# Routing 8192 tokens to pairs of experts: places from products on TensorE, logits from the unscaled residual, an earlier first product

## The chip, the cores and the metric

One core of a Trainium2 chip runs the whole program. The metric is the device time in microseconds (us) of one execution.

## What is computed

Input: 8 sequences of 1024 rows of 128 channels. A frequency-domain attention and convolution block gives a residual; its layer norm is the input of a mixture of eight experts, and a second layer norm gives the output. For the change only the routing matters:

```python
x = _layernorm(x + attn(x))                       # 8192 rows, D = 128
d2 = sum(xs*xs) + sum(centroid*centroid) - 2*(xs @ centroid.T)
dist = sqrt(maximum(d2, 1e-12))
w, sel = top_k(dist, 2); w = softmax(w)           # the two farthest centroids
we[row, sel] = w
for e in range(8):
    h = silu(xs @ Wg[e] + bg[e]) * (xs @ W1[e] + b1[e])
    out += we[:, e:e+1] * (h @ W2[e] + b2[e])
x = _layernorm(x + out)
```

## The kernel before, in words

**Phase 1** (`phase1`, lines 161 to 994) works batch by batch (8 batches of 8 tiles of 128 rows), as a software pipeline whose last part is a `tail()` on each engine. The normed rows go to `rows_dram`, their transposes times the centroids give the logits `lg`, and GpSimd gives the squared norms `sq`. Each engine has its own program in an order written out by hand, with counting semaphores between them; an engine waits in order, and everything behind a wait waits too. VectorE's tail (lines 863 to 928) runs: the first of the two top-one searches over the 48 tiles of batches 0 to 5 (`top_two`, line 1014), residual and statistics of the last batch (L892 to L899), an inverse root by a Newton chain of small linked operations (L901 to L909), four of the eight scalings of the last batch (L913; ScalarE does the other four, L703), copies, the second search, the one-hots `OH` of the 28 pairs of experts (`pair_rows`, L1048 to L1058), then for three chunks of 16 tiles a scan and a rank (`pair_sums` L1070, L1071; `pair_ranks` L1078 to L1080). In the loop GpSimd makes the inverse root (L971 to L983). SP stores the rows (L325, L327).

**Routing** (`route`, L1083 to L1341) is the first part of phase 2, a block that starts when all engines have ended phase 1. VectorE: both searches for the last 16 tiles, their pair one-hots, the last scan and rank, the running totals of the pairs (L1170, L1171), which tile holds rows of which pair (L1172 to L1175), each row's place (L1193 to L1202), the step tables' one-hots (L1205 to L1213), then in four quarters one-hots of the place's high and low part (L1225 to L1228). TensorE multiplies these, which inverts the permutation (L1327); `steptab` (L1240 to L1245) and `idx` (L1251) come out, and `placed` is signalled. GpSimd builds the rows' weights `we` (L1281 to L1284), splits the biases into a high and a low part (L1287, L1289), stores and reloads them into row 127 of the weights (L1292, L1296), then waits for `placed` and gathers the first four tiles (L1302). SP stores `we` (L1341). VectorE waits for all of these stores ahead of `idx`.

**Experts** (`experts`, L1354 on): tile k of the permuted rows is gathered by GpSimd four steps ahead, transposed on TensorE (L1478), copied by ScalarE into `xT` (L1538), split by ScalarE into `xh` (L1522) and by GpSimd into `xl` (L1425). A step t does two units (a tile with an expert): products for gate and value (`up`, L1447), Silu (L1533), product h (L1620), transposes (L1455), products down (L1465), accumulation (L1631). Offsets of a step are loaded from `steptab` into each engine's registers. The order on TensorE in a step is: transpose of tile t+2, gate products, value products, transposes of step t-1, down products of step t-2. So transposes 0, 1 and 2 stand ahead of the first product.

## Time and profile before

| | |
|---|---|
| median of 3 runs (lowest, highest) | 600.55 us (600.13, 600.82) |
| profiled execution: its time, its span | 602.22 us, 600.2 us |
| mean granted TensorE clock | 0.93 |
| busy over the span: TensorE, weight load | 507.4 us (85%), 477.5 us (80%) |
| busy: VectorE, ScalarE, GpSimd | 395.2 (66%), 341.3 (57%), 287.3 (48%) |
| moved by DMA in the first of 40 slices | 231 GB/s |

The page's picture of 40 slices of 15 us, in tenths:

```profile
PE   3868999999998540087999999999999999999990
DVE  2579879889989888981334346555564646666663
POOL 0132534544553100615444444577777777754443
PEclk9979989999999855578999999999999999999996
```

Slices 0 to 13 are phase 1, 14 to 17 its tail and the routing, the rest the experts. An engine's digit is its busy share of the slice, PEclk the granted clock. PE is TensorE, PEld its weight load, DVE VectorE, ACT ScalarE, POOL GpSimd, SP the sync engine; an engine's name with a q is its queue.

### The profile page before, as it was taken

To read this page: it belongs to the slowest core of one execution; us is meant where nothing else is said; L and a number is where in the kernel's file an instruction comes from. 1 tells how busy PE (TensorE), PEld (TensorE's weight loads), DVE (VectorE), ACT (ScalarE), POOL (GpSimd) and SP (SyncE) were. 2 spreads that over 40 slices of the span, in tenths; PEclk is the share of its full clock that TensorE was granted. 3 is DMA by queue.
4 is the path that set the end of the run, shared out by engine and by line. 5 is a ranking of instruction groups with operands and counts; after the bars stand their busy time and mean duration, and the time that the engine had idled before them with its cause. 6 is when DMAs were issued, how large, how long until landed. Compare 5 with 4: busy or idle time off the path is not lost.

```text
span 600.2 us, 13796 instructions
## 1 busy us (share of the span) xinstructions
PE 507.4 (85%) x4090; PEld 477.5 (80%) x4090; DVE 395.2 (66%) x1121; ACT 341.3 (57%) x721; POOL 287.3 (48%) x414
## 2 busy tenths in 40 slices
PE   3868999999998540087999999999999999999990
PEld 3766887887887430076999999999999999999990
DVE  2579879889989888981334346555564646666663
ACT  3366868878877402035555555666666575755661
POOL 0132534544553100615444444577777777754443
PEclk9979989999999855578999999999999999999996
DMA  8241246146232110201000000111111111100000
GB/s 231 66 128 49 51 115 162 45 121 163 78 85 72 35 35 2 21 9 24 20 20 20 20 18 18 29 33 35 35 39 33 34 37 38 35 26 19 19 23 31
DMA packets 48975, 31.16 MB, mean 52 GB/s; under 512 B 14251, under 2 KB 46582, under 8 KB 48918
## 3 DMA queue, kind: packets, MB, share of 16 engines
q1 hardware_dynamic: 43974, 20.87, 13.6%
q0 software_dynamic: 4224, 8.75, 5.3%
q10 hardware_dynamic: 720, 0.82, 0.5%
q8 instruction: 31, 0.51, 0.3%
q14 instruction: 26, 0.21, 0.1%
HBM read 21.73 MB, written 8.69 MB: 51 GB/s over the span
## 4 chain that ended last, share of the span: by engine, by line
PE 52%; DVE 3%; issue 3%; POOL 2%; DMA 1%; POOLq 0%; ACT 0%; DVEq 0%
PE ps L1447 25%; PE ps L1465 17%; PE ps L1455 8%; PE ps L1478 1%; DMA bias_parts<-blo 1%; POOL wo L1282 0%; DMA xs<-rows_dram,idx 0%; POOL we L1284 0%; POOL out_dram L1414 0%; POOL blo L1289 0%; POOL xs L1302 0%; POOL bhi L1287 0%; DVE Lc L1071 0%; POOL we L1281 0%; DVE xs L1631 0%
## 5 line engine op out<-in xcount | busy, mean ns | idle before, releaser
L1447 PE MATMUL ps<-wts,xh 128*128 x620 | 154.2, 332 | 1.3 <-issue 1.2
L1620 DVE TENSOR_TENSOR h<-ps,sg 128x684 f32<-128x684 f32 x78 | 67.6, 866 | 91.1 <-PE ps L1447 90.8
L1465 PE MATMUL ps<-w2s,hT 115*128 (+1 forms) x930 | 116.5, 274 | 0.3 <-DVE xs L1631 0.3
L1425 POOL TENSOR_TENSOR xl<-xT,xh 127x128 fp32r<-127x128 f32 x155 | 67.9, 457 | 98.6 <-ACT xh L1522 98.5
L1465 PEld LDWEIGHTS ps<-w2s,hT 115*128 115x128 f32 (+1 forms) x930 | 109.9, 191 | 0.6 <-issue 0.6
L1447 PEld LDWEIGHTS ps<-wts,xh 128*128 128x128 f32 x620 | 104.6, 191 | 1.8 <-issue 1.7
L1447 PE MATMUL ps<-wts,xl 128*128 x310 | 99.4, 321 | 0.0
L1533 ACT ACTIVATE sg<-ps 128x684 f32<-128x684 f32 x78 | 57.7, 739 | 67.2 <-PE ps L1447 67.2
L1542 ACT ACTIVATE hT<-ps 114x768 f32<-114x768 f32 x78 | 63.0, 808 | 56.5 <-PE ps L1455 56.5
L1631 DVE SCALAR_TENSOR_TENSOR xs<-ps,xs 128x128 f32 x155 | 54.3, 351 | 50.6 <-PE ps L1465 47.6
L1414 POOL DMA_INDIRECT out_dram<-xs,idx x64 | 62.9, 982 | 25.8 <-issue 17.6
L1455 PE MATMUL ps<-cr,h 128*114 128x128 f32 x465 | 63.4, 272 | 0.3 <-issue 0.3
L1410 POOL DMA_INDIRECT xs<-rows_dram,idx x60 | 58.1, 969 | 9.1 <-issue 4.4
L1447 PEld LDWEIGHTS ps<-wts,xl 128*128 128x128 f32 x310 | 58.8, 190 | 0.0
L1455 PEld LDWEIGHTS ps<-cr,h 128*114 128x114 f32 x465 | 54.5, 134 | 2.3 <-issue 0.5
L1522 ACT ACTIVATE xh<-xT 127x128 fp32r x155 | 39.1, 301 | 2.0 <-ACT xT L1538 0.9
L742 DVE SCALAR_TENSOR_TENSOR YI<-XF,dw,YI 128x432 f32<-128x432 f32 (+5 forms) x48 | 37.0, 772 | 0.6
L967 POOL TENSOR_TENSOR Pb<-Sb,rs 128x512 f32<-128x512 f32 x16 | 19.2, 1198 | 28.7 <-DVE rs L830 28.6
L742 DVE SCALAR_TENSOR_TENSOR YR<-XF,dw,YR 128x448 f32<-128x448 f32 (+5 forms) x48 | 30.9, 644 | 1.7
L1507 ACT ACTIVATE xs<-xs,nrm,y 128x128 f32<-128x128 f32 x64 | 27.8, 483 | 7.3 <-DVE nrm L1603 7.3
L971 POOL TENSOR_TENSOR y<-ve,cm 128x8 f32<-128x8 f32 x7 | 11.6, 1664 | 37.8 <-DVE vh L763 37.8
L961 POOL TENSOR_TENSOR wts<-st,wts 128x684 f32 (+1 forms) x8 | 13.1, 1640 | 27.8 <-ACT wts L636 27.8
(280 smaller groups left out, 870.3 us busy)
## 6 DMA issues: line engine op xcount, KB each, us to landing
xt<-_attn_hidden_states_dram SPq DMA_DIRECT2D x8, 512.0 KB, 6.0
xres<-_attn_hidden_states_dram SPq DMA_DIRECT2D x7, 512.0 KB, 5.3
rows_dram<-x1s SPq DMA_DIRECT2D x7, 512.0 KB, 3.7
w2s<-in_L_ffn_W_dram SPq DMA_DIRECT2D x8, 171.0 KB
st<-in_L_ffn_Wg_dram SPq DMA_DIRECT2D x8, 171.0 KB, 3.1
st<-in_L_ffn_W_dram SPq DMA_DIRECT2D x8, 171.0 KB, 3.6
stl<-in_L_ffn_Wg_dram SPq DMA_DIRECT2D x8, 171.0 KB, 3.7
stl<-in_L_ffn_W_dram SPq DMA_DIRECT2D x8, 171.0 KB, 4.2
```

The costliest lines, as they stand in the source:

```text
L742: ins = v.scalar_tensor_tensor(out=y[:, :, k:n], in0=src, scalar=w, in1=y[:, :, k:n], op0=ALU.mult, op1=ALU.add)
L1410: v.indirect_dma_start(xs[:, k, 0:RD], None, rows, bass.IndirectOffsetOnAxis(idx[:, k:k + 1], 0)).then_inc(gat[k % GATS], 16)
L1414: v.indirect_dma_start(out_rows, bass.IndirectOffsetOnAxis(idx[:, k:k + 1], 0), xs[:, k, 0:D], None).then_inc(s["scattered"], 16)
L1425: v.tensor_tensor(xl[0:D - 1, i % 2, u, :], xT[0:D - 1, bass.ds(off[u], P)], xh[0:D - 1, i % 2, u, :].bitcast(F32), ALU.subtract).then_inc ...
L1447: mm = pe.matmul(ps[:, 2 * w + u, 0:HF], a[:, t % 2, u, :], wflat[:, bass.ds(w1[u] + (b + w * HF), HF)], start=(k == 0), stop=(k == 2))
L1455: mm = pe.transpose(ps[0:HG, 4 + u, k * P:(k + 1) * P], h[:, t % 2, u, k * HG:(k + 1) * HG], ident)
L1465: mm = pe.matmul(ps[:, low(t) + u, 0:D], hT[0:n, t % 2, u, k, :], w2flat[0:n, bass.ds(w1[2 + u] + k * D, D)], start=(k == 0), stop=(k == 2))
L1522: nc.scalar.activation(xh[0:D - 1, i % 2, u, :], xT[0:D - 1, bass.ds(off[u], P)], ACT.Copy).then_inc(s["xh_done"], 1)
L1533: nc.scalar.activation(sg[:, 0:units(t), :], ps[:, 0:units(t), 0:HF], ACT.Silu).then_inc(s["sg_done"], 1)
L1542: nc.scalar.activation(hT[0:HG, b % 2, 0:n, :, :].rearrange("p u k m -> p u (k m)"), ps[0:HG, 4:4 + n, 0:3 * P], ACT.Copy).then_inc(s["hT_ ...
L1620: v.tensor_tensor(h[:, t % 2, 0:units(t), :], ps[:, 2:2 + units(t), 0:HF], sg[:, 0:units(t), :], ALU.mult).then_inc(s["h_done"], 1)
L1631: v.scalar_tensor_tensor(out=row, in0=ps[:, low(c) + u, 0:D], scalar=xsflat[:, bass.ds(off[2 + u], 1)], in1=row, op0=ALU.mult, op1=ALU.add ...
```

## The change

- **Places.** Ranks and totals no longer come from scans. TensorE multiplies `OH` by a triangle (rank within a tile), by a vector of ones (counts of each tile), and by the identity (its transpose `oht`); small products of the counts give totals and each (pair, tile)'s first place, split in two two-byte parts and spread into `R`, and `oht` times `R` gives each row's first place. Pairs are laid out in rounds, so four multiplications make `OH` in place of nineteen. Tables of need and of steps are made with products too. Most constants are packed as two-byte numbers, and all but the first 137 columns are loaded later, on SP.
- **Last batch.** TensorE transposes and multiplies the unscaled residual `xt`; the scale and the mean are applied to the logits (`nc8`). GpSimd makes the inverse root. ScalarE scales all eight tiles into `xlast`. The second search and the pair one-hots of the 48 tiles follow the statistics at once. ScalarE makes the early tiles' square roots.
- **Moved.** Weights of the rows in two parts (48 and 16 tiles), on GpSimd for more of their steps; the bias split to GpSimd's tail of phase 1 and its stores to SP; three memsets from VectorE to GpSimd; `idx` ahead of the tables (`tabled`); waits for the stores from VectorE to GpSimd.
- **First product.** Transposes 1 and 2 follow the first gate and value products; three gathers go ahead instead of four.

```diff
+def pair_columns():
+    return [tuple(sorted((a, (a + d) % E))) for d in range(1, E // 2 + 1) for a in range(E if d < E // 2 else E // 2)]
...
@@ phase1, SP @@
+                if X and not Y:
+                    sp.dma_start(cr[:, g["c2"]["gblk"][0]:], g["cst2"][:, g["c2"]["gblk"][0]:]).then_inc(rest_in, 16)
+                    sp.dma_start(braw[:, 0:HF], g["bg"]).then_inc(s["bias_in"], 16)
+                    sp.dma_start(braw[:, HF:], g["b1"]).then_inc(s["bias_in"], 16)
...
+                for k, part in enumerate((bhi, blo)):
+                    sp.wait_ge(s["bias_split"], k + 1)
+                    sp.dma_start(parts[k], part[:, :].bitcast(F32)).then_inc(bias_out, 16)
+                sp.wait_ge(bias_out, 32)
+                for k in range(2):
+                    sp.dma_start(wts[D - 1:D, :, 2 * k * HF:2 * (k + 1) * HF].bitcast(F32), parts[k:k + 1]).then_inc(bias_out, 16)
                 sp.wait_ge(s["last_x1"], TB)
-                sp.dma_start(rows_t[B - 1][:, :, 0:D], xres[:, :, :]).then_inc(s["rows_out"], 16)
+                sp.dma_start(rows_t[B - 1][:, :, 0:D], xlast[:, :, :]).then_inc(last_out, 16)
...
-            sp.wait_ge(s["rows_out"], 16 * B)
+            sp.wait_ge(rows_out, 16 * (B - 1))
@@ TensorE @@
-            pe.matmul(ps[:, 6, 0:E], ones[:, :], cT2[:, :], start=True, stop=True).then_inc(s["prep_mm"], 1)
+            pe.matmul(ps[:, 6, 0:E], ones[:, :], cT2[:, :], start=True, stop=True)
+            pe.matmul(ps[:, 6, E:2 * E], ones[:, :], cT[:, 0:E], start=True, stop=True).then_inc(s["prep_mm"], 1)
...
+                for h in range(2):
+                    pe.wait_ge(s["zs_done"], 2 * (B - 1) + h + 1)
+                    for j in range(4):
+                        mm = pe.transpose(ps[:, h, j * P:(j + 1) * P], xt[:, 4 * h + j, :], ident)
+                    mm.then_inc(s["t_done"], 1)
@@ ScalarE, tail @@
+                act.wait_ge(w_early, 1)
+                for m, root in ((g["m1"], g["s1"]), (g["m2"], g["s2"])):
+                    nc.scalar.activation(root[:, 0:EARLY * CT], m[:, 0:EARLY * CT], ACT.Sqrt).then_inc(s["sqrt_early"], 1)
                 act.wait_ge(s["last_rstd"], 1)
+                for j in range(TB):
+                    nc.scalar.activation(xlast[:, j, :], xt[:, j, :], ACT.Identity, bias=nl[:, j:j + 1], scale=yl[:, j:j + 1]).then_inc(s["last_x1"], 1)
@@ VectorE, tail, behind the statistics @@
+                v.tensor_scalar(vl[:, :], mvl[:, :, 1], EPS, None, ALU.add).then_inc(s["last_seed"], 1)
+                v.tensor_scalar(vhl[:, :], mvl[:, :, 1], EPS, 0.5, ALU.add, ALU.mult).then_inc(s["last_seed"], 1)
+                top_two(nc, g, 0, EARLY * CT, link, True)
+                dve.sem_inc(w_early, 1)
+                pair_rows(nc, g, 0, EARLY, link)
...
+                link(v.tensor_tensor(last, ps[:, 6, 0:TB * E].rearrange("p (j e) -> p j e", j=TB), yl[:, :].unsqueeze(2).broadcast_to((P, TB, E)), ALU.mult))
+                v.tensor_tensor(last, last, nc8[:, :, :], ALU.add).then_inc(s["lg_ev"], 1)
@@ GpSimd, tail, behind squares(B - 1) @@
+                pool.wait_ge(s["bias_in"], 32)
+                v.tensor_copy(bhi[:, :], braw[:, :]).then_inc(s["bias_split"], 1)
+                pool.wait_ge(s["bias_split"], 1)
+                v.tensor_tensor(blo[:, :], braw[:, :], bhi[:, :].bitcast(F32), ALU.subtract).then_inc(s["bias_split"], 1)
+                pool.wait_ge(s["last_seed"], 2)
+                v.tensor_tensor(yl[:, :], vl[:, :], cm[:, :], ALU.pow).then_inc(s["last_root"], 1)
...
@@ pair_rows @@
+    for d in range(1, E // 2 + 1):
+        w = E if d < E // 2 else E // 2
+        ins = v.tensor_tensor(OH[:, c0:c1, at:at + w, :], maskT[:, 0:w, lo:hi].rearrange("p a (c t) -> p c a t", t=CT),
+                              maskT[:, d:d + w, lo:hi].rearrange("p a (c t) -> p c a t", t=CT), ALU.mult)
@@ route, VectorE @@
+            dve.wait_ge(s["tri_cp"], EARLY)
+            link(v.tensor_tensor(prod[:, 0:EARLY, :, :], trs[:, :, :, :], OH[:, 0:EARLY, :, :], ALU.mult))
+            dve.wait_ge(s["counts"], 2)
+            v.tensor_copy(cntb[:, EARLY, :], cnt[:, EARLY * BLK:]).then_inc(s["counts_cp"], 1)
...
+            dve.wait_ge(s["firsts"], 1)
+            link(v.tensor_copy(hl[:, :, 0], V))
+            link(v.tensor_tensor(hl[:, :, 1], V, hl[:, :, 0], ALU.subtract))
...
             for k in (14, 7):
-                link(v.tensor_tensor(posm[:, :, 0:k, :], posm[:, :, 0:k, :], posm[:, :, k:2 * k, :], ALU.add))
+                link(v.tensor_tensor(prod[:, :, 0:k, :], prod[:, :, 0:k, :], prod[:, :, k:2 * k, :], ALU.add))
...
+            dve.wait_ge(s["places"], 1)
@@ in the quarters @@
+                if c == 1:
+                    dve.wait_ge(s["upto"], 1)
+                    link(v.tensor_tensor(upos[:, :], upto, need[:, :], ALU.mult))
+                    v.tensor_tensor(uhot[:, :, :], short("unit").unsqueeze(1).broadcast_to((P, 4, UPAD)), upos[:, :].unsqueeze(2).broadcast_to((P, 4, UPAD)),
+                                    ALU.is_equal).then_inc(s["unit_hot"], 1)
...
@@ route, ScalarE @@
+            for c in range(EARLY):
+                act.wait_ge(s["tri"], c + 1)
+                nc.scalar.activation(trs[:, c, :, :].rearrange("p a t -> p (a t)"), ps[:, 2 + c, 0:NPAIR * CT], ACT.Copy).then_inc(s["tri_cp"], 1)
+            for c in range(EARLY):
+                turned(c, (0, 1, 6)[c])
+            act.wait_ge(s["late"], 1)
+            for m, root in ((m1, s1), (m2, s2)):
+                nc.scalar.activation(root[:, TE:NT], m[:, TE:NT], ACT.Sqrt).then_inc(s["sqrt"], 1)
...
@@ route, GpSimd @@
+            weights(0, 0, TE, s["weights_early"])
+            pool.wait_ge(s["weights_early"], 1)
+            v.memset(xh[96:P, :, :, :].bitcast(F32), 1.0).then_inc(prep, 1)
...
+            weights(1, TE, NT, s["weights_late"])
@@ route, TensorE @@
+            for c in range(EARLY):
+                mm = counts(c)
+            mm.then_inc(s["counts"], 1)
+            for c in range(EARLY):
+                tri(c, 2 + c)
+            for c in range(EARLY):
+                turned(c, (0, 1, 6)[c])
...
+            totalled(0, EARLY)
...
@@ experts @@
+            pool.wait_ge(weights_out, 16 * B)
+            pool.wait_ge(rows_out, 16 * (B - 1))
+            pool.wait_ge(last_out, 16)
+            pool.wait_ge(placed, 1)
+            for k in range(GATS - 1):
+                gather(k)
...
+                if t < 0 or t >= 1:
+                    if t != -1:
+                        turn_in(k)
...
                     up(t, 0, w1[t]).then_inc(s["g_done"], 1)
+                if t == 0:
+                    turn_in(1)
```

The functions that the diff calls: `counts(c)` is four products of one column, `turned(c, bank)` four of 128, `tri(c, bank)` one of 448, `totalled` four of one column for each chunk, all of two-byte data; `weights(k, lo, hi, done)` is w2, two weightings and their sum for the tiles lo to hi; `turn_in(k)` waits for gather k and transposes tile k.

## Rows read from the trace of the kernel before

**Rows 1.** Windows: start and end, width, busy us (x instructions) per engine, granted clock, DMA.
```profile
280.00:600.00 320.00, 304.95 (x2366) 302.50 (x2364) 172.03 (x528) 184.19 (x429) 185.36 (x272) 0.98 0.10 28
```

**Rows 2.** Waits from 196 to 282 us: total, times, longest.
```profile
POOL xs L1302 <- DVE idx L1251: 11.3, 1, 11.3
```

**Rows 3.** Timeline of VectorE: start, us, line, operation, out<-in [idle before].
```profile
204.34 0.64 DVE L899 BATCH_NORM_AGGREGATE mvl<-bn 128x2 f32<-128x6 f32 x8
...
210.64 0.55 DVE L1031 SCALAR_TENSOR_TENSOR dist<-oh,dist 128x384 f32<-128x384 f32 x1
...
214.17 0.86 DVE L1048 TENSOR_TENSOR maskT<-oh 128x384 bf16<-128x384 f32 x1
...
227.76 0.90 DVE L1080 TENSOR_REDUCE rank<-rtmp 128x16 f32<-128x448 f32 x1
229.20 0.29 DVE L1033 TENSOR_TENSOR dist<-lg,cn 128x128 f32<-128x128 f32 x1 [0.54 <-PEq L176]
...
267.54 0.23 DVE L1251 SCALAR_TENSOR_TENSOR idx<-inv 128x64 uint32<-128x64 f32 x1
```

**Rows 4.** Timeline of VectorE, one two-byte comparison of a quarter.
```profile
256.10 1.21 DVE L1226 TENSOR_TENSOR lohot<-io,lob 128x2048 bf16<-128x2048 bf16 x1
```

**Rows 5.** Timelines of GpSimd and VectorE where they meet.
```profile
95.51 1.64 POOL L961 TENSOR_TENSOR wts<-st,wts 128x684 f32 x1 [1.63 <-ACT wts L636]
...
95.92 1.68 DVE L742 SCALAR_TENSOR_TENSOR YI<-XF,dw,YI 128x416 f32<-128x416 f32 x1
...
249.96 1.61 POOL L1289 TENSOR_TENSOR blo<-braw,bhi 8x684 fp32r<-8x684 f32 x1
...
250.25 1.41 DVE L1197 TENSOR_TENSOR pos<-pos,rank 128x64 f32<-128x64 f32 x1
```

**Rows 6.** Timeline of GpSimd: the inverse root in the loop, and weights.
```profile
108.00 1.64 POOL L971 TENSOR_TENSOR y<-ve,cm 128x8 f32<-128x8 f32 x1 [5.23 <-DVE vh L763]
...
112.68 0.20 POOL L983 TENSOR_TENSOR nmr<-c,ya 128x8 f32<-128x8 f32 x1
...
242.84 1.07 POOL L1281 TENSOR_TENSOR we<-oh,r_w 128x512 f32<-128x512 f32 x1 [6.36 <-DVE r_w L1186]
243.87 2.85 POOL L1282 TENSOR_TENSOR wo<-oh,r_w 128x512 f32<-128x512 f32 x1
```

**Rows 7.** Timeline of ScalarE: a switch of tables, scalings, copies out of PSUM.
```profile
95.30 1.28 ACT L639 ACT_TABLE_LOAD   x1
96.60 0.63 ACT L639 ACTIVATE Sb<-Sb 128x512 f32<-128x512 f32 x1
...
198.70 3.18 ACT L694 ACTIVATE x1s<-xres,nmr,y 128x128 f32<-128x128 f32 x8
202.69 1.09 ACT L698 ACTIVATE x1T<-ps 128x512 f32<-128x512 f32 x2 [0.81 <-PE ps L513]
```

**Rows 8.** Timeline of TensorE: two-byte products of 156 and of 128 columns.
```profile
255.64 3.28 PE L1319 MATMUL ps<-uhot,ulhs 64*1 64x156 bf16 x24 [12.32 <-DVE ulhs L1213]
...
265.06 2.05 PE L1327 MATMUL ps<-hihot,lohot 128*128 128x128 bf16 x16 [0.27 <-DVE hihot L1228]
```

**Rows 9.** The stores of `we` on SP: timeline, and the line's landing times.
```profile
248.82 5.12 SPq L1341 DMA_DIRECT2D rows_dram<-we  x8
...
DMA to landing us min/median/max: 2.2/3.0/3.8
```

**Rows 10.** Start of the experts: timelines of TensorE and ScalarE, a window.
```profile
270.72 0.33 PE L1478 MATMUL ps<-cr,xs 128*128 128x128 f32 x1 [1.78 <-DMA xs<-rows_dram,idx]
...
274.81 0.93 PE L1447 MATMUL ps<-wts,xh 128*128 x2 [1.17 <-issue]
...
276.92 0.74 ACT L1533 ACTIVATE sg<-ps 128x684 f32<-128x684 f32 x1 [2.05 <-PE ps L1447]
...
274.00:277.00 3.00, 2.19 (x8) 2.20 (x9) 0.00 (x0) 0.95 (x2) 1.56 (x3) 0.56 0.10 25
```

**Rows 11.** Timeline of TensorE in the prologue.
```profile
15.91 0.60 PE L344 MATMUL ps<-cT,ones 128*128 128x8 f32 x2 [1.55 <-ACT cT L566]
```

More of the change, by code:

```diff
@@ new lines, in resident_constants @@
+    twice = twice.copy()
+    twice[:, 0:NPAIR] += np.eye(NPAIR)
+    twice[:, 32:32 + NPAIR] += np.eye(NPAIR)
+    parts["glast"] = rows_of(twice)
+    first, end = np.full((64, P), BIG), np.full((64, P), -BIG)
+    inc = np.zeros((64, E // 2))
+    for h in range(2):
+        r = slice(32 * h, 32 * h + NPAIR)
+        first[r, 64 * h:64 * h + NT] = np.arange(NT) * P
+        end[r, 64 * h:64 * h + NT] = np.arange(NT) * P + P
+        for p, pair in enumerate(cols):
+            for e in pair:
+                if e // 4 == h:
+                    inc[32 * h + p, e % 4] = 1
@@ L109, in resident_constants @@
+    parts["io4"] = halves(np.tile(np.repeat(np.arange(P), 4), (P, 1)).astype(float))
+    parts["tiles"] = halves(np.tile(np.arange(NT), (P, 1)).astype(float))
     return parts
@@ L1264, in _ @@
[L1264 removed]
+                act.wait_ge(s["high"], c + 1)
+                nc.scalar.activation(hihot[:, part, 0, :, :], hieq[:, part, :, :], ACT.Copy, scale=con("part")).then_inc(s["high_place"], 1)
         @block.gpsimd
```

611 lines of the change are left out of this document (311 added, 300 removed).

## The prediction, made before the changed kernel was run

> **What bounds the kernel now.** I read the page first, then stretches, waits and the timeline of each engine between the two phases. In the experts' phase TensorE is busy for 305 of 320 us at a granted clock of 0.98 (2.4 GHz nearly throughout) [rows 1]: the change leaves that loop alone, so those 320 us stay. Between the phases TensorE is mostly idle, and the wait that ends last is GpSimd's for `idx`: 11.3 us on VectorE [rows 2]. So the path is VectorE's. Its timeline [rows 3] gives the landmarks: statistics of the last batch end at 204.98, its scans and ranks end at 228.66, the routing block starts at 229.20, and `idx` is written at 267.77. A microsecond taken out of that chain is a microsecond of span. The profiled execution took 602.22 us (span 600.2); the median of the runs shown is 600.55, so I subtract 1.67 at the end.
>
> **Tail of phase 1, on VectorE.** Removed from it: the Newton chain of twelve small operations, four scalings, the copy of x1T, three scans with nine following operations. Added: two seeds (0.25), one second logits operation. What is left behind the statistics is the second top-two of 48 tiles, 214.17 - 210.64 = 3.53 us, the mask (0.86, and about 0.35 for its three repeated rows), four pair products in place of nineteen small ones (384 two-byte elements at the rate of the 2048-element comparison, 1.21 us or 0.57 ns each [rows 4], plus 0.1: about 1.1 together) and two logits operations, 0.6. That would end at 204.98 + 0.25 + 3.53 + 1.2 + 1.1 + 0.6 = 211.7.
>
> **What the moved bias split costs there.** GpSimd now does it behind its squares, at about 198, beside VectorE's first top-two. The trace shows what such a meeting costs: a VectorE operation on 416 elements with two SBUF inputs, which should be near the 0.55 us of 384 elements [rows 3], takes 1.68 when GpSimd's 1.64 us subtraction started before it, and the addition of 64 elements takes 1.41 because it has to let `blo` end at 251.57 [rows 5]. The second is the very operation that is moved, so its 1.61 us falls on the top-two almost whole: I take 1.7 us for the pair, with 0 (they miss) and 2.75 (both whole, with the 1.14 of `bhi`'s cast taken into the bound as an estimate of the same kind of width) as ends. Statistics then end at 206.7 and VectorE's phase at 213.4.
>
> **The last rows go over ScalarE and SP.** The inverse root is GpSimd's now. In the loop the same seven operations take from 108.00 to 112.88, 4.9 us [rows 6], so bias and scale are ready at 206.95 + 4.9 = 211.85. VectorE's second top-two ends at 210.5, and ScalarE's two early square roots behind it are done by 211.1 (about 0.25 each), so they cost nothing; their cover is the root chain. Then ScalarE scales all eight tiles alone: eight such operations took 3.18 [rows 7], until 215.1. SP issues the row store (0.4) and the block ends; its landing is no longer waited for here. With the 0.5 us that the boundary took before (228.66 to 229.20), the routing block starts at 216.0 against 229.2. **ScalarE, not VectorE, sets this end.** The two bias stores and loads are on SP before it, behind 201, and have 10 us to land; without that cover they would cost two trips of some 3 us. The transposes and logit products of the last batch run unscaled while VectorE is in the statistics.
>
> **Routing block, VectorE's order, counted from its start.** Top-two of 16 tiles: fourteen operations of 0.29 with 0.03 between them, 4.5; signal and pair rows 1.3: 5.8. Now a wait: ScalarE must have copied three triangular products. TensorE makes twelve counts, three products of 448 columns, twelve turned blocks and twelve totals; a small two-byte product costs 0.137 in a run of 24 and 0.128 in one of 16 [rows 8], I take 0.12 for the narrower ones: 1.45 + 1.1 + 1.45 + 1.45, so the totals are there at 5.6, and ScalarE's three copies at half a microsecond each (two of 512 columns took 1.09 [rows 7]) end at 7.5. VectorE stalls 1.7. Early products 1344 elements 0.85, counts copy 0.2, reciprocal 0.4, last total after four more products 0.7, late products 0.65 (PSUM input, 448 elements at the 1.2 ns of the 384-element operation, 0.55 [rows 3], plus start): 10.4. The first places need eight single-precision passes, here 0.12 each: 11.3, a stall of 0.9. Split 0.4, spread 0.55, bounds and presence 0.45, two halvings 0.9, reduction 0.95, reciprocal 0.2, five operations to `lob` 1.0: 15.7. Between the first places and the reduction, TensorE makes sixteen place products (2.0) and ScalarE turned blocks, bounds and weights, all hidden by the halvings; if they are late, the place addition waits. The four quarters of one-hots are as before, 4096 elements each at 0.57 ns, 9.4: 25.1. Within them the presence, `upos` and `uhot` cost 0.95, and a wait for `upto`, which stands behind the first sixteen inverse products, 0.7: 26.8. The last sixteen inverse products 2.05 [rows 8] with latency 2.3, copy and `idx` 0.55: 29.65. The tables (1.7) come behind `idx` and run beside the first gather.
>
> The old block took 267.77 - 229.20 = 38.6. Gone are its scan and ranks, the wide base product with its single-precision halvings, half of the one-hot units, and the tables ahead of `idx`.
>
> **GpSimd's weights beside it.** Differences, products, eight-wide weights and the memsets taken from VectorE now run from about 11.4 of this block (the late square roots stand on ScalarE behind its three copies, three turned blocks, 1.65, and a switch of tables, 1.3), meeting VectorE's two-input operations. Alone GpSimd's list is some 6.5 us: for the early 48 tiles three wide steps of 0.85 and two small ones, four memsets of up to 0.5, and the same for 16 tiles. Half as much again for the meetings, and the weights end at about 21; their stores, 0.64 each and 3.8 to land at worst [rows 9], at about 26, under the 32 of `idx`.
>
> So `idx` stands at 216.0 + 29.65 + 2.5 = 248.15 in place of 267.77: 19.6 us saved, 13.2 in the tail of phase 1 and 6.4 in routing.
>
> **First product.** It stood 274.81 - 267.77 = 7.04 behind `idx`, the first transpose 2.95 behind it, and 1.17 went into loading offsets after the third [rows 10]. Now it needs the first tile only: 2.95 + 0.3 + 1.2, about 4.45. But the second transpose comes behind its first half, and ScalarE does copy, split and a table load of 1.28 before the Silu, which before was ready and waited for TensorE at 276.92. That Silu comes 9.2 to 10.1 behind `idx`, ended 9.8 before. Of the 2.6 us on TensorE I therefore count 0.5; ends 2.6 saved and 1 lost (the fourth gather is now issued behind the first subtraction).
>
> **Prologue.** A product more (two passes, 0.60 for two [rows 11]) adds up to 0.6 ahead of the first transforms; 278 KB less of constants to load ahead of the first transposes gives back up to 1.2, at the 231 GB/s of the page's first slice. I take 0.3 saved, with 0.6 lost and 0.9 saved as ends. The rest of the constants, three SP issues in the first step of the loop, lies beside compute.
>
> **Sum.** 602.2 - 19.6 - 0.5 - 0.3 = 581.8 in the profiled execution, 580.1 for the median; I say 580.
>
> **Table loads, trace against notes.** In the loop the load starts at 95.30 and the Exp behind it at 96.60 [rows 7]: 1.30 us for a switch, nothing more. That price is in the steps above. By the Trainium skill (ScalarE: Activation LUTs, What ACT_TABLE_LOAD costs) a switch is a load of 1283 ns and a drain of about 1380 ns; the row does not show the drain.
>
> **Rivals.** (1) *The forecast's path*, 580, likeliest: 0.67.
> (2) *GpSimd's weights end last.* If each of its steps goes at 2.85 for 1.07, its 6.5 us become 17.5, from 227.4 to 244.9, and the stores land 5.1 later at 250.0, 1.9 behind my `idx`: 582. For it, the row of 2.85; against it, that blocking is mutual and VectorE waits often in this block. 0.12.
> (3) *The early first product counts whole.* The granted clock was 0.56 from 274 to 277 [rows 10], against 0.98 over the experts' phase [rows 1], after the lull before the first product. If the lull is short enough for full clock to hold, the first half step takes 0.9 less and all of the start counts: 577. 0.11. The rows do not say which.
> (4) *A switch costs load and drain.* Two switches stand ahead of the bounds and the late weights, one ahead of the Silu: if a switch blocks for a second stretch as long as its load, 1.28 more each, and half of it hides: 582. The switch row nearly excludes it: 0.01. (The page named above gives this mechanism.)
> (5) *Slower.* The weights of (2), starved at the port, stretched by more than 5.4: from 227.4, 6.5 x 5.4 + 5.1 us of stores reach 267.6, where `idx` was. Above that factor the kernel is slower than before; at a factor of 6 they land at 271.5, which gives 603. The dearest ratio in the trace is 2.7: 0.03.
> (6) *Same mechanism, dearer hops*: some dozen crossings between engines that I priced at 0.1 or less cost 0.5 to 1 each, single-precision rates on the new two-byte operations: 588 to 596, 0.05.
> (7) *It does not shorten the path*: something else held the experts back. Nothing in the waits says so: 0.01.
>
> **Range and chances.** Downward, from 580: the split misses (1.7), no blocking in routing (2.5), start whole (2.1), prologue (0.6): 573. Upward: blocking whole (1.1 and 1.9), two-byte operations at single-precision rate (2.2), hops (1.2), start and prologue (2.4): 589. That holds (1) to (4) and part of (6). A measurement of this kernel tells about 0.2% from no change. Faster 0.96: all but (5) and (7); same 0.01; slower 0.03.
>
> **What would show it.** Right: the routing block starting near 216 behind eight ScalarE scalings; VectorE's first top-two with one operation of about 2 us; a stall of about 1.7 before the early product; `idx` near 248 and first product 4.5 behind it; TensorE's loop of experts unchanged. Wrong: a block start set by VectorE or SP; GpSimd's first gather waiting for `we` stores; `hieq` quarters longer than 2.4 us; a lower clock in the experts' phase.

## The result, and the profile after

The changed kernel takes 583.12 us (median of 4 runs, 580.71 to 584.92), the one before 600.68 us on the same chip (4 runs, 600.13 to 602.06): a ratio of 0.9717, 95% interval 0.9684 to 0.9749, 17.6 us less. Predicted were 580 us and a range of 573 to 589. The profiled execution took 584.92 us, its span is 582.4 us, its mean granted clock 0.93.

| stretch of the profiled executions, us | before | after | predicted change | measured change |
|---|---|---|---|---|
| start to VectorE's last `VT` | 196.53 | 199.39 | -0.3 | +2.86 |
| tail: to the routing block's first operation | 32.67 | 18.80 | -13.2 | -13.87 |
| routing: to the end of `idx` | 38.57 | 29.69 | -6.4 | -8.88 |
| start: to the transpose of tile 5 | 17.79 | 19.38 | -0.5 | +1.59 |
| experts behind it, to the end | 314.6 | 315.1 | 0 | +0.5 |
| span | 600.2 | 582.4 | -20.4 | -17.8 |

These five stretches, read from the timelines of VectorE and TensorE, are used for every kernel below. The tail and routing together gave 22.75 us where 19.6 were predicted; phase 1 and the start took back 4.45.

The busy tenths of the profile's page, in 40 slices of 14.6 us:

```profile
PE   3768989999999856769999999999999999999990
DVE  1569778899899888813434447464645556666663
POOL 0142525545535533054454454776776776754453
PEclk9769889999999965689999999999999999999996
```

TensorE's lull between the phases had digits of 5, 4, 0, 0 and now has none below 5. New, and not a matter of the edit as far as one sees here: the third digit of PEclk is 6, the granted clock fell in the prologue.

**Tail.** Timeline of VectorE in the changed kernel (start, us, line, operation, shapes, idle before):

```profile
199.39 0.46 DVE L944 SCALAR_TENSOR_TENSOR VT<-ps,al,xln 128x64 f32<-128x64 f32 x2 [1.09 <-PE ps L572]
...
200.98 0.93 DVE L1115 TENSOR_SCALAR dist<-dist 128x384 f32<-128x384 f32 x1
201.95 0.55 DVE L1116 TENSOR_REDUCE r_m<-dist 128x48 f32<-128x384 f32 x1
202.53 1.28 DVE L1117 TENSOR_TENSOR eq<-dist,r_m 128x384 f32<-128x384 f32 x1
...
215.63 0.23 DVE L981 TENSOR_TENSOR lg<-lg,nc 128x64 f32<-128x64 f32 x1
218.19 0.29 DVE L1113 TENSOR_TENSOR dist<-lg,cn 128x128 f32<-128x128 f32 x1 [2.34 <-PEq L236]
```

Timeline of GpSimd beside it:

```profile
200.95 0.74 POOL L1041 CAST bhi<-braw 8x684 fp32r<-8x684 f32 x1
201.78 1.62 POOL L1043 TENSOR_TENSOR blo<-braw,bhi 8x684 fp32r<-8x684 f32 x1
...
213.24 0.69 POOL L1058 TENSOR_TENSOR nl<-c,yal 128x8 f32<-128x8 f32 x1
```

And of ScalarE:

```profile
213.97 3.18 ACT L780 ACTIVATE xlast<-xt,nl,yl 128x128 f32<-128x128 f32 x8 [0.68 <-POOL nl L1058]
218.14 1.28 ACT L1293 ACT_TABLE_LOAD   x1 [0.99 <-PEq L236]
219.44 0.24 ACT L1293 ACTIVATE r_ew<-r_df 128x48 f32<-128x48 f32 x1
...
222.38 1.37 ACT L1308 ACTIVATE trs<-ps 128x448 bf16<-128x448 f32 x3
```

Two operations of the first search are long, each while one of the two halves of the bias split is under way; the reduction between them, at 0.55, is not. VectorE is through at 215.86 and then idle for 2.34 us; ScalarE's eight scalings end last, at 217.15, and the block begins 1.04 later, with SP's issue of the row store (0.41 us from 217.18) in between.

**Routing.** VectorE again, to be set against [rows 3 to 5]:

```profile
223.88 0.85 DVE L1212 TENSOR_TENSOR prod<-trs,OH 128x1344 bf16<-128x1344 bf16 x1
...
227.73 0.18 DVE L1225 CAST hl<-ps 112x16 bf16<-112x16 f32 x1 [1.50 <-PE ps L1406]
...
228.15 1.37 DVE L1227 TENSOR_TENSOR R<-hl,cr 112x512 bf16<-112x512 bf16 x1
229.45 1.01 DVE L1231 TENSOR_SCALAR mxs<-cr,bb 64x128 f32<-64x128 f32 x1
...
233.44 0.42 DVE L1243 TENSOR_SCALAR hii<-posi 128x64 int32<-128x64 int32 x1
...
239.42 0.16 DVE L1267 TENSOR_TENSOR upos<-ps,need 128x4 bf16<-128x4 f32 x1
...
247.66 0.22 DVE L1273 SCALAR_TENSOR_TENSOR idx<-inv 128x64 uint32<-128x64 f32 x1
```

The early product has no idle time before it: its inputs are ready. The one real stall is 1.50 us, for the first places. `upos` does not wait for `upto` either: the products for it end at 239.39, 0.03 ahead.

**Start of the experts.** Timelines of GpSimd, TensorE and ScalarE in the order of time, and three windows (start and end, width, busy us of each engine, granted clock, DMA), to be set against [rows 10]:

```profile
248.87 1.18 POOL L1526 DMA_INDIRECT xs<-rows_dram,idx  x1 [14.17 <-DVE idx L1273]
...
253.18 0.90 PE L1569 MATMUL ps<-wts,xh 128*128 x2 [1.11 <-ACT xh L1658]
...
256.62 1.28 ACT L1669 ACT_TABLE_LOAD   x1
...
257.92 0.74 ACT L1669 ACTIVATE sg<-ps 128x684 f32<-128x684 f32 x1
...
258.93 0.30 PE L1578 MATMUL ps<-cr,xs 128*128 128x128 f32 x1 [1.78 <-ACT sg L1669]
```

```profile
254.00:256.00 2.00, 2.00 (x9) 1.94 (x8) 0.00 (x0) 0.28 (x1) 0.96 (x1) 0.50 0.16 41
...
258.00:260.00 2.00, 1.07 (x7) 1.10 (x8) 0.87 (x1) 1.34 (x4) 1.14 (x3) 1.00 0.14 35
260.00:262.00 2.00, 2.00 (x10) 1.93 (x9) 0.00 (x0) 0.91 (x2) 1.27 (x2) 0.54 0.00 0
```

The first product stands 5.3 us behind the end of `idx` in place of 7.04, but the Silu behind it 10.04 in place of 9.15: a table load stands directly ahead of it, and TensorE then waits 1.78 us for it. The first gather begins 0.99 us behind `idx`; before it was 0.28.

Three questions followed: whether the change lengthened phase 1, what the start's parts are, and whether the blocked operations of tail and routing are what I took them for.

### The profile page after: what moved, and what is told of

Same layout as the page of the kernel before. It is cut to its first block, busy times and chain, and to the rows that moved or that the text cites. A ratio compares the mean times of both kernels' runs of the same rounds, so it can differ in the third digit from the quotient of the medians.

```text
span 582.4 us, 13894 instructions
## 1 busy us (share of the span) xinstructions
PE 514.3 (88%) x4161; PEld 486.5 (84%) x4161; DVE 371.0 (64%) x1045; ACT 350.7 (60%) x743; POOL 289.1 (50%) x422
## 3 DMA queue, kind: packets, MB, share of 16 engines
q0 software_dynamic: 4096, 8.66, 5.5%
## 4 chain that ended last, share of the span: by engine, by line
PE 55%; DVE 4%; issue 1%; ACT 1%; DMA 0%; POOL 0%; DVEq 0%; ACTq 0%; POOLq 0%
PE ps L1569 25%; PE ps L1594 17%; PE ps L1584 9%; PE ps L1578 1%; PE ps L1427 1%; DMA xs<-rows_dram,idx 0%; DVE lohot L1257 0%; POOL out_dram L1530 0%; PE ps L1441 0%; PE ps L1406 0%; DVE hieq L1256 0%; DVE xs L1763 0%; ACT xs L1641 0%; DVE R L1227 0%; DVE hihot L1259 0%
## 5 line engine op out<-in xcount | busy, mean ns | idle before, releaser
L1530 POOL DMA_INDIRECT out_dram<-xs,idx x64 | 62.9, 982 | 26.2 <-issue 17.5
L1526 POOL DMA_INDIRECT xs<-rows_dram,idx x64 | 62.4, 975 | 23.9 <-DVE idx L1273 14.2
L1019 POOL TENSOR_TENSOR Pb<-Sb,rs 128x512 f32<-128x512 f32 x16 | 19.2, 1199 | 28.7 <-DVE rs L902 28.6
```

The source lines that it names most:

```text
L1526: v.indirect_dma_start(xs[:, k, 0:RD], None, rows, bass.IndirectOffsetOnAxis(idx[:, k:k + 1], 0)).then_inc(gat[k % GATS], 16)
L1530: v.indirect_dma_start(out_rows, bass.IndirectOffsetOnAxis(idx[:, k:k + 1], 0), xs[:, k, 0:D], None).then_inc(s["scattered"], 16)
```

## The experiments

Each starts from the changed kernel, unless it says otherwise. Spreads are lowest to highest run; the kernel before ran beside each of them and stood at 599.93 to 600.63 us. The groups ran on different chips, so medians of different groups are compared only roughly.

| kernel | median, us (runs; spread) | ratio to before, 95% interval | to `VT` | tail | routing | start | span |
|---|---|---|---|---|---|---|---|
| the change again | 583.83 (6; 578.9 to 585.1) | 0.9717 [0.9679, 0.9756] | 195.45 | 18.82 | 29.67 | 17.94 | 577.0 |
| transposes as before | 579.82 (6; 579.0 to 582.5) | 0.9668 [0.9635, 0.9701] | 193.03 | 18.80 | 29.69 | 19.44 | 576.1 |
| Silu table early | 577.23 (6; 574.3 to 579.8) | 0.9606 [0.9572, 0.9640] | 196.49 | 18.80 | 29.71 | 17.13 | 577.0 |
| Silu early, tables held back | 577.52 (5; 576.8 to 578.7) | 0.9609 [0.9584, 0.9633] | 195.92 | 18.81 | 29.66 | 16.58 | 575.9 |
| idle products | 575.64 (6; 574.7 to 576.8) | 0.9587 [0.9556, 0.9618] | 191.54 | 18.80 | 29.70 | 19.32 | 574.4 |
| the kernel before, idle products | 596.66 (7; 595.9 to 597.5) | 0.9936 [0.9913, 0.9959] | 191.19 | 32.68 | 38.57 | 18.10 | 595.4 |
| bias split earlier | 579.37 (4; 578.7 to 583.6) | 0.9673 [0.9632, 0.9714] | 195.46 | 17.51 | 29.69 | 17.99 | 575.8 |
| and scalings shared | 578.33 (4; 578.1 to 580.8) | 0.9631 [0.9598, 0.9663] | 198.83 | 16.97 | 29.68 | 17.54 | 577.9 |
| constant weights | 577.24 (4; 574.3 to 581.5) | 0.9598 [0.9552, 0.9644] | 197.68 | 18.81 | 27.79 | 19.20 | 578.6 |
| Silu, split, scalings | 574.43 (5; 573.7 to 575.2) | 0.9558 [0.9534, 0.9583] | 194.19 | 16.99 | 29.70 | 16.99 | 572.6 |
| and idle products | 571.09 (6; 570.3 to 572.8) | 0.9504 [0.9480, 0.9527] | 192.36 | 16.98 | 29.70 | 17.18 | 570.9 |
| and gathers placed as before | 571.99 (6; 570.7 to 572.6) | 0.9527 [0.9488, 0.9567] | 192.07 | 16.98 | 29.69 | 16.75 | 570.2 |

The stretches are of the profiled execution alone. Tail and routing repeat within 0.05 us; the time to `VT` lies between 193.0 and 199.4 in the six profiles of kernels whose phase 1 is the same, and the start scatters too. Medians of kernels without idle products therefore carry that draw, and an edit is judged by its stretch first.

### Was phase 1 longer because of the change?

The change, run again without an edit:

> The changed kernel itself, unedited, as the measure for the three kernels beside it. Its four runs so far lie between 580.71 and 584.92 us, a spread of 4.2, while the kernel before spreads by 0.7 in its first three. Theory A: the spread is TensorE's clock. In the profiled run the granted clock was 0.50 from 18 to 24 us and 0.55 from 39 to 42, where the kernel before had 1.00, and phase 1 came out 2.86 us later at the first operation of its tail. Then runs with a fast prologue have that operation near 196.5 and runs with a slow one near 199.4, and the rest (tail, routing, start) agrees within 0.5 us. Theory B: the later prologue is work that the change added (a product, a later load) and is there in every run. Expected median 583, range 580.5 to 585.

Its stretch to `VT` was 195.45, 3.9 less than in the first profile and 1.1 less than before the change. So the 2.86 us are mostly not the change's. The start did not repeat within the expected 0.5: 17.94 for 19.38.

What goes with the time to `VT` is the granted clock, in two places. The first batch's statistics come at 60.2 to 64.6 us in the six profiles of this phase 1, with granted clocks of 0.50 to 0.89 in the two windows shown below. From there to the second batch's it takes 23.4 to 23.7 us where the granted clock from 80 to 100 us is 0.91 to 0.94 (four of the six, and the kernel before), and 21.5 to 21.7 where it is 1.00 (two). Behind that every profile of every kernel takes 21.6 us for each of the next four batches: all of the scatter of phase 1 lies ahead of about 110 us.

Next, idle products on TensorE, in two gaps of the prologue:

```diff
+            for _ in range(8):
+                pe.matmul(ps[:, 7, 0:P], ident, ident, start=True, stop=True)
             pe.wait_ge(s["prep_cp"], 10)
...
+                if Y and not T:
+                    pe.wait_ge(s["v_ev"], 2)
+                    for _ in range(6):
+                        pe.matmul(ps[:, 7, 0:448], ident, cs[:, 0:448], start=True, stop=True)
```

> TensorE gets idle products in two gaps of the prologue: eight of 128 columns behind the preparing transposes and six of 448 columns ahead of the first transposes of step 1; nothing reads them. Theory A (the later and more scattered prologue is the clock's doing): the clock stays at 1.00 from 15 to 60 us, the first operation of the tail comes at 196.5 or earlier, 2 to 4 us are saved and the spread of the runs falls to under 1 us. Theory B (the prologue is later because of added work): the clock stays up but the tail starts within 0.5 us of 199.4.

The same lines in the kernel before the change:

> The kernel before the change, with the same idle products in the two gaps of the prologue as in e_warm (eight of 128 columns, six of 448; nothing reads them). In e_warm the first operation of the tail came at 191.5 us, in the kernel before at 196.5, in the unedited changed kernel at 199.4 and 195.5. Theory A (the length of phase 1 is set by when TensorE's clock rises in the prologue, and the change has no part in it): the kernel before gains as much, its tail starts at 191 to 192.5 and its time falls by 4 to 6 us to about 595. Theory B (the change made the prologue dearer and the idle products only repair that): the kernel before gains under 1.5 us.

Windows of the prologue (columns as above; the granted clock is the third number from the right), first before:

```profile
18.00:24.00 6.00, 4.73 (x22) 4.43 (x22) 2.62 (x9) 1.19 (x2) 1.01 (x1) 1.00 0.32 94
...
36.00:42.00 6.00, 5.81 (x42) 5.41 (x41) 2.16 (x7) 3.41 (x7) 2.44 (x2) 0.77 0.30 90
```

after:

```profile
18.00:24.00 6.00, 4.72 (x22) 4.43 (x22) 3.16 (x9) 1.30 (x3) 1.10 (x1) 0.50 0.36 108
...
36.00:42.00 6.00, 5.82 (x29) 5.44 (x28) 1.03 (x3) 2.66 (x5) 2.39 (x2) 0.52 0.12 37
```

after, with idle products:

```profile
18.00:24.00 6.00, 4.72 (x36) 3.94 (x34) 4.36 (x11) 3.01 (x6) 0.96 (x1) 1.00 0.46 140
...
36.00:42.00 6.00, 6.00 (x48) 5.79 (x48) 4.72 (x11) 4.58 (x9) 0.00 (x0) 1.00 0.40 119
```

In the profile of the change TensorE is at the lower level (0.5 of 2.4 GHz, 1.2 GHz) through all of 18 to 24 us and nearly all of 36 to 42. With the idle products, 191.54 and 191.19 us to `VT`: **at a full clock in these windows the change's own part in phase 1 is 0.35 us in one profile of each**, and that is not told from none: the first transposes wait for the load of `Vs`, and start at 8.70 to 10.24 us in the twelve profiles of changed kernels, at 9.03 and 9.12 in the two of the kernel before. The two kernels stand 21.0 us apart (596.66 and 575.64, on two chips), close to the 20.5 that I had predicted between before and after.

In the kernel before, the same edit gave 3.7 us by the median and 5.3 in the profile's stretch; in the changed kernel 8.2 and 3.9. For the kernel before, the stretch came as expected and the median just short of the 4 to 6 us; for the changed kernel the gain was more than the expected 2 to 4 us and the spread, 2.2 us, did not fall under 1. In both, the granted clock from 80 to 100 us was 1.00 too, and the step behind the first statistics took 21.3 us. Why the unedited change lost more to it than the kernel before is not settled: with the same code in phase 1 the windows from 18 to 24 us read 0.50, 0.77 and 0.81 in three profiles.

### The parts of the start

Transposes 1 and 2 put back ahead of the first product (the three conditions around `turn_in` taken out):

> The order of the first three transposes alone is undone: all three stand ahead of the first product again. In the profiled changed kernel the transpose of tile 5 comes 19.4 us behind idx, before it was 17.8. Theory A (ScalarE's chain of copy, split, table load and Silu is what step 1 waits for, and the early first product puts the second copy behind it): with the order undone the first product moves back by about 2 us, the Silu of step 0 comes no later than 10.5 us behind idx and step 1 is 0 to 1 us earlier or the same, so the time is the same within 1 us. Theory B (the early first product is worth its 2.6 us on TensorE): the time rises by 2 to 2.6 us.

The table load of the Silu brought forward, by a Silu of one column ahead of ScalarE's experts' loop:

```diff
+            nc.scalar.activation(g["warm"][:, :], g["m1"][:, 0:1], ACT.Silu)
             sent = 0
```

> One Silu of one column is added on ScalarE ahead of the experts' loop, so that the table load of 1.28 us, which stands between the split of tile 1 (ends 256.61) and the Silu of step 0 (starts 257.92), runs in the lull before idx. Theory A (ScalarE's chain sets step 1): Silu and step 1 come 1.3 us earlier, and since TensorE's lull is shorter its clock may hold, so 1.3 to 3 us are saved. Theory B (the first steps are set by gathers or by TensorE's own clock): the load is gone and the time is the same within 0.5 us.

Timeline of TensorE and ScalarE with the transposes as before:

```profile
249.56 0.94 PE L1569 MATMUL ps<-wts,xh 128*128 x2 [1.16 <-issue]
...
251.67 0.74 ACT L1663 ACTIVATE sg<-ps 128x684 f32<-128x684 f32 x1 [2.10 <-PE ps L1569]
```

and of ScalarE with the early table load:

```profile
241.67 1.28 ACT L1645 ACT_TABLE_LOAD   x1
...
253.66 0.72 ACT L1671 ACTIVATE sg<-ps 128x684 f32<-128x684 f32 x1
```

With the transposes ahead, the first product stands 8.04 behind the end of `idx` (241.52) and the Silu 10.15, against 5.25 and 9.97 in the rerun of the change: 2.8 us on the first product are 0.2 us on the Silu, and 0.6 on the fourth transpose (11.62 and 10.98).

The medians can't price this edit: the old order's stands 4.0 us below the rerun's, where neither theory had a gain of more than 1. The two profiled executions are 0.9 us apart in span, with 2.4 less to `VT`, which the edit does not touch, and 1.5 more in the start.

With the table early, the Silu stands 8.66 behind `idx` (244.99) and no load stands between. In all five kernels with the early table the start is 16.6 to 17.2; in the six with the late one and the new order it is 17.5 to 19.4. So the late Silu, which I had named, is what kept the early product from counting: with the transposes as before it waits 2.10 us for the product, in the new order for its table. The old order with an early table was not run.

The means of the two groups (16.93, 18.56) differ by 1.6 us, and the clock has a part in it. From 9 to 17 us behind `idx` the granted clock is 0.92 to 1.00 in the three late ones of 17.5 to 18.0 and 0.66 to 0.79 in the three of 19.2 to 19.4, and 0.87 to 1.00 in the five early ones: at a like clock the early table is worth 0.9 us (17.82 and 16.93), and the rest goes with the clock.

Now the gather that begins 0.7 us later than before. First VectorE's seven table operations, which follow `idx` at once, are held back until GpSimd has passed the first gather:

```diff
                 gather(k)
+                if k == 0:
+                    pool.sem_inc(g["gone"], 1)
...
             dve.wait_ge(s["tables"], 1)
+            dve.wait_ge(g["gone"], 1)
```

> After with ScalarE's Silu table loaded early and VectorE's step tables held back until GpSimd has issued the first gather. Question: why does the first gather start 0.99 us behind the end of idx (before: 0.28), and does it matter? Theory A, VectorE's seven small table operations, which now run directly behind idx, hold GpSimd's gather up: with them held back the gather starts 0.3 behind idx, and the first transpose 3.1 to 3.2 behind it in place of 3.86; the tables come some 1.3 us later, so the offsets, and the first product, may be as late as before: first product 5.3 to 5.8 behind idx. Theory B, the distance comes from GpSimd's own waits or its place in another function: still 0.99. Phase 1, tail 18.8 and routing 29.7 as in after. Time: 576 to 580, by the draw of phase 1.

Then, in the kernel with all four edits, the waits and gathers are moved back to the end of GpSimd's routing program:

> The kernel with all four edits (571.09 us median), with one more: the four waits and the first three gathers stand at the end of GpSimd's program for routing, as before the change, and not at the start of its program for the experts. Theory A, the late start of the first gather comes from its place behind a jump into another part of the program: it starts 0.28 behind the end of idx instead of 0.98, the first transpose stands 2.9 to 3.2 behind in place of 3.85, and the time is 0.7 lower, about 570.4. Theory B, it comes from the waits themselves (three for stores stand ahead of the one for idx): still 0.98, first transpose at 3.85, time 571. Everything else as in the kernel with four edits: tail start 191.5 to 192.4, tail 17.0, routing 29.7.

VectorE with the tables held back, and GpSimd:

```profile
244.17 0.22 DVE L1275 SCALAR_TENSOR_TENSOR idx<-inv 128x64 uint32<-128x64 f32 x1
245.25 0.31 DVE L1285 COPY ut<-ps 1x156 f32<-1x156 f32 x1 [0.85 <-POOLq L1542]
```

```profile
245.38 1.18 POOL L1529 DMA_INDIRECT xs<-rows_dram,idx  x1 [14.15 <-DVE idx L1275]
```

VectorE stands idle for 0.85 us and the gather still begins 0.99 behind `idx`. In its old place it begins at 239.72, 0.98 behind. Both theories with a cause fell. What is left of what I had named is GpSimd's own waits, three for stores ahead of the one for `idx`; that was not tried, since the waits are needed, and the 0.7 us stay unexplained.

### The blocked operations

The bias split moved ahead, to GpSimd's first step of phase 1 (a step with `X` and without `Y` is the first), behind its scaling of `Pb`; there it runs at 35.46 to 38.20 us. The expectation for all parts together, further below, puts it beside the last step, which is wrong:

```diff
+                if X and not Y:
+                    pool.wait_ge(s["bias_in"], 32)
+                    v.tensor_copy(bhi[:, :], braw[:, :]).then_inc(s["bias_split"], 1)
+                    pool.wait_ge(s["bias_split"], 1)
+                    v.tensor_tensor(blo[:, :], braw[:, :], bhi[:, :].bitcast(F32), ALU.subtract).then_inc(s["bias_split"], 1)
```

> In the changed kernel GpSimd splits the biases in the first step of phase 1 instead of in its tail. In the profiled changed kernel VectorE's first top-two has two operations of 0.93 and 1.28 us where 0.36 and 0.56 were taken before. Theory A (the split blocks VectorE at a shared port): both are back at 0.36 and 0.56, and the tail from the first operation behind TensorE's attention products to the routing block takes 17.5 us instead of 18.8. Theory B (they are longer for another reason): the tail stays at 18.8.

The same, and three of the last eight scalings on VectorE, which was idle there:

```diff
-                for j in range(TB):
+                for j in range(5):
                     nc.scalar.activation(xlast[:, j, :], ...
...
+                for j in range(5, TB):
+                    v.tensor_scalar(xlast[:, j, :], xt[:, j, :], yl[:, j:j + 1], nl[:, j:j + 1], ALU.mult, ALU.add).then_inc(s["last_x1"], 1)
```

> As e_bias, and VectorE scales three of the last batch's tiles behind its logits, ScalarE only five. Theory A (ScalarE's eight scalings and the row store behind them end phase 1, VectorE waits 2.3 us): the tail takes 0.4 to 0.6 us less than in e_bias, about 17.0. Theory B (the end is set by SP or the boundary itself): as in e_bias, 17.5.

GpSimd's weights replaced by a constant 0.5 (`w2`, `we` and `wo` are not worked out; one memset for each of the two parts):

> In the changed kernel GpSimd leaves out the rows' weights: it writes the constant 0.5 in place of w2, both weightings and their sum. Routing takes 29.7 us from its first operation to the end of idx. Theory A (these operations block VectorE at the shared port; the profile has the spread at 1.37, the bounds at 1.01, the first comparison at 0.86 us): they fall to about 0.6, 0.25 and 0.68 and routing takes 2.0 to 2.5 us less, 27.3 to 27.7. Theory B (they are that long by their shapes, since both broadcast their input): routing takes 29.2 or more.

VectorE's first search with the split moved:

```profile
197.05 0.36 DVE L1116 TENSOR_SCALAR dist<-dist 128x384 f32<-128x384 f32 x1
...
198.03 0.56 DVE L1118 TENSOR_TENSOR eq<-dist,r_m 128x384 f32<-128x384 f32 x1
```

VectorE in routing with constant weights:

```profile
226.46 0.69 DVE L1227 TENSOR_TENSOR R<-hl,cr 112x512 bf16<-112x512 bf16 x1
227.06 0.31 DVE L1231 TENSOR_SCALAR mxs<-cr,bb 64x128 f32<-64x128 f32 x1
...
230.35 0.20 DVE L1243 TENSOR_SCALAR hii<-posi 128x64 int32<-128x64 int32 x1
```

Both are shown. Without the split beside it the search's two operations take 0.36 and 0.56 in place of 0.93 and 1.28, and the tail is 1.3 us shorter. Without the weights, `R` takes 0.69 for 1.37, `mxs` 0.31 for 1.01, `hii` 0.20 for 0.42, `hib` behind it 0.20 for 0.33 and the first `hieq` 0.69 for 0.86. These five make up the whole 1.90 us by which routing is shorter, just under the 2.0 to 2.5 expected. GpSimd's memsets cost nothing: the two halvings of `prod` take 1.04 in both kernels, beside memsets in the one and alone in the other, and `mxs` takes its 0.31 beside a memset. Sharing the scalings takes another 0.54 us off the tail, which shows that ScalarE set its end; now VectorE's three do, at 214.77 in that profile, 1.03 ahead of the block.

By the Trainium skill (GPSIMD Engine Reference, Specifications) GpSimd's way to SBUF is shared with VectorE and contends with VectorE's operations of two SBUF inputs and with those in a two-port mode. The rows agree with it: `blo` blocked an operation of two SBUF inputs. `mxs` and the first search's L1115 have one tensor input and were blocked too (the page's other case, though no row names the mode), the reduction at 201.95 and the 64-element addition with a PSUM input at 233.18 (0.22 us with the weights beside it and without) were not.

### The parts together

> After with three edits together: Silu table loaded early, bias split behind VectorE's last loop step's work instead of beside the first search, three of the eight last scalings on VectorE. No idle products in the prologue. Expected: tail 17.0 us (18.80 in after), routing 29.7, idx to the transpose of tile 5 about 17.1. Phase 1's length is drawn as before (193 to 199 to the start of the tail), so the time is 575 to 578, with the wide scatter of after. If instead the gains of the parts were only luck of the draw, the median is at 580 or above.

> The same three edits together with the idle products on TensorE in the prologue. Expected: tail starts at 191.5, takes 17.0; routing 29.7; idx to tile 5 about 17.1; experts 315.1: span 191.5 + 17.0 + 29.9 + 17.1 + 315.1 = 570.6, time about 573, and a scatter of 1 to 2 us. This would be about 10 us under after and 27 under before. If the clock in the experts' start depends on the prologue's rather than on the lull before it, idx to tile 5 is at 19 and the time at 575.

The first came out 0.6 us under the expected 575 to 578, the second 2 us under the expected 573 with a span of 570.9 for 570.6; so the gains of the parts add up: tail and start came out as said. **571.09 us is 12.0 us below the change and 29.5 below the kernel before** (the last beside it on the same chip, 600.63); the tail is 16.98 and the start 17.18. The two spans differ by 11.5: the stretches give 7.0 for the time to `VT` (199.39, 192.36), 1.8 for the tail, 2.2 for the start and 0.4 for the rest. Without the idle products it is 574.43, and its five runs lie within 1.5 us although nothing was done for the clock of the prologue: the scatter of the earlier kernels is not in every one of them.

The split is not free in its new place once the clock is full. VectorE's four copies into `XL` in the changed kernel with idle products, and with all four edits, and TensorE behind the latter:

```profile
36.63 0.49 DVE L856 COPY XL<-XF 128x64 f32<-128x64 f32 x4 [2.89 <-ACT XF L675]
36.95 1.37 DVE L857 COPY XL<-XF 128x64 f32<-128x64 f32 x4 [2.88 <-ACT XF L676]
38.38 2.05 PE L476 MATMUL ps<-XL,qwT 128*128 128x128 f32 x16 [0.41 <-DVE XL L857]
```

GpSimd's subtraction ahead of the second step's weights, which began at 33.53, now stands behind the split, from 36.35 to 37.98, beside these copies. TensorE is 0.32 us behind the other profile at 32 us and 1.00 behind at 42, so about 0.7 us of the time to `VT` (192.36 for 191.54) is the split's, and the profile with the gathers placed as before shows the same copies (1.36) and the same wait (0.40). In the three profiles of the split without idle products the copies take 0.48 to 0.49, and no such cost is seen.

## Why the prediction was right, and where it was off

The sign and the mechanism held: the path between the phases was VectorE's, and what was taken out of it came out of the span. Predicted 580, measured 583.12, inside the range. By its steps:

- **Split beside the first search.** 1.7 us taken, 1.3 measured, in two operations and not in one of about 2 us; the price was read from the right rows, the overlap was not quite whole.
- **Inverse root on GpSimd**: 4.9 taken, 4.44 measured (209.49 to 213.93). **Eight scalings**: 3.18 taken, 3.18 measured. Boundary with SP's issue: 0.9 taken, 1.04 measured. "ScalarE, not VectorE, sets this end" was right. The tail was predicted 0.7 us too long.
- **Early product waits 1.7 for the triangular copies**: wrong, no wait at all. The step that failed is the price of TensorE's small products and of the copies. I took 0.12 us for every one; the twelve products of one column for the totals have a stretch of 0.41 between their first start and the next group's, where I had 1.45. The counts took 1.11 for 1.45 and the turned blocks 1.28 for 1.45, so the totals were through at 4.0 us and not 5.6; three copies took 1.37 in place of 1.5, so that they ended at 223.75, 5.6 us into the block and not 7.5.
- **Stall for the first places**: 0.9 taken, 1.50 measured. The early end of the first step is partly paid back here: VectorE now waits for TensorE's eight single-precision passes, which take 1.65 us from the start of one to the end of the last, where I had priced 0.12 each.
- **Wait for `upto`**: 0.7 taken, none measured, for the same reason. The eight products of at most four columns that it stands behind take 0.38 us in all.
- **Weights at the port**: 2.5 taken, 1.90 measured. GpSimd's list ended 16.5 us after the block's start where I had said 21, so rival (2) and the slower (5) did not occur: its own steps were stretched little, 1.32 for 0.85 at worst.
- The quarters, the operations for `need`, `upos` and `uhot`, and the last inverse products went as priced: 9.4, 0.95 and 2.85 taken, 13.5 us measured from `hieq` to the end of `idx`.
- **Start**: 0.5 us saved was predicted, 1.59 lost in the first profile, 0.15 in the rerun. "Silu 9.2 to 10.1 behind `idx`" held (10.04, 9.97), and the early product counted little, as taken. The first product stands 5.3 behind `idx` where I had 4.45. What I had not seen is the first gather's 0.7 us, and the scatter that comes with the clock at the low level in the first steps.
- **Prologue**: 0.3 saved was predicted; at equal clock 0.35 was lost in one profile of each, within the scatter of the loads. The load of the first constants gave nothing back that shows, since the first transposes wait for `Vs` and not for them: they start at 9.53 us in place of 9.03, and at 8.70 to 10.24 in other profiles. The 2.86 us of the profile are a draw, which no step of the sum had, for I had read one execution as if phase 1 always took 196.5 us.
- **Table loads.** In the changed kernel the activation starts 1.30 us after the load wherever its inputs are ready, as at 218.14 and 256.62. Rival (4) did not occur. By the Trainium skill (ScalarE: Activation LUTs, What ACT_TABLE_LOAD costs) about 1380 ns of drain would be added; the rows show none.

So the two misses of size have opposite signs. Tail and routing gave 3.2 us more than said, from small products and waits priced too dear; phase 1 and start gave 5.3 less than said, and of that 2.5 us went away in phase 1 once the clock was held (2.86 and 0.35). The experts' 0.5 us were not followed up. That `idx` ended at 247.88 where I had 248.15 is luck: phase 1 was 2.86 us late and tail and routing 3.15 us shorter than said.

## What to carry to other kernels

Ahead of a comparison of two kernels, look at the granted clock of the same early windows in both: where it differs, the same code can differ by several microseconds, and a few idle products in the gaps of TensorE make both kernels comparable, and here faster too. When a first product is pulled forward, follow the chain to the first operation that uses it: a table load there let 2.8 us on the first product become 0.2 on the Silu, and one early activation of a single column moved the Silu forward by 1.3. Work moved to GpSimd is paid by VectorE where their operations meet, memsets excepted here; move it to where VectorE works from PSUM or waits, and then ask what it pushes behind itself, as the split pushed a subtraction onto VectorE's copies.

## What the runs showed of the hardware beyond what was expected

Some of TensorE's two-byte products of one to four columns follow each other very closely. Its timeline in the changed kernel:

```profile
239.09 0.17 PE L1434 MATMUL ps<-need,cr 128*128 128x4 bf16 x1
239.11 0.17 PE L1435 MATMUL ps<-need,cr 128*128 128x3 bf16 x1
239.14 0.17 PE L1434 MATMUL ps<-need,cr 128*128 128x4 bf16 x1
```

Each lasts 0.17 us, but they start 0.03 us apart, at a granted clock of 0.50; the 0.12 that I took from products of 128 columns was four times too much for these and for the totals. It was not for all: the twelve counts, of one column too but with blocks of `OH` for weights, start 0.09 us apart, with weight loads of 0.21 us where those here take 0.10. What makes that difference was not tested. By the Trainium skill (TensorE: Matmul & The Clock Gate, Wait — 56ns, not 53.3ns?) starts never come closer than about 25 ns however few the columns: the rows agree. With 0.03 for the totals and for the products of `upto`, the wait of 0.7 would not have stood in the sum, and of the 1.7 about 0.6 would have been left.

The other surprise is the prologue: the same instructions, in the same order, at a granted clock between 0.50 and 0.85 from 18 to 24 us and between 0.52 and 0.89 from 36 to 42, and 193.0 to 199.4 us until the tail.
